# A grouped attention of 128 steps in a fused kernel: rolled rows with a drain each, or one unrolled line with another order and with the squares summed on ScalarE

## The reference, cut to what matters

```python
# x: (4, 256, 256) after layer norm; ctx: (4, 1601, 256); 16 query heads, 4 key/value heads, 128 per head
q = rms_norm((x @ Wq).reshape(4, 256, 16, 128), q_norm_w)
k = rms_norm((ctx @ Wk).reshape(4, 1601, 4, 128), k_norm_w)
v = (ctx @ Wv).reshape(4, 1601, 4, 128)
# each k and v head serves 4 query heads
probs = softmax(einsum('bqhd,bkhd->bhqk', q, k) / 128 ** 0.5)
x = x + einsum('bhqk,bkhd->bqhd', probs, v).reshape(4, 256, 2048) @ Wo
```

## Time and profile before

| what | value |
|---|---|
| median of 3 runs | 2012.29 us (2007.18 to 2012.59) |
| the profiled execution: time, span | 2008.84 us, 2007.0 us |
| busy in the span | PE 1739.7 us (87%), DVE 1303.9 us (65%), ACT 980.6 us (49%), POOL 615.8 us (31%) |
| granted TensorE clock, mean | 0.955 |
| the block: from its first DMA to its last addition | 659.9 to about 1922 us |

### The profile page before, as it was taken

The page is one execution under the profiler, slowest core; times in us unless marked ns, Lnnn a source line. Parts: engine busy times, 40 slices in busy tenths (PEclk is TensorE's granted clock), DMA queues, the critical chain, the costliest instruction groups (busy, mean ns, idle before and its releaser), DMA issues. The chain is left out here.

```text
span 2007.0 us, 32922 instructions
## 1 busy us (share of the span) xinstructions
PE 1739.7 (87%) x10769; PEld 1524.8 (76%) x10772; DVE 1303.9 (65%) x2618; ACT 980.6 (49%) x2010; POOL 615.8 (31%) x482
## 2 busy tenths in 40 slices
PE   5787599999999589998989998989998979999944
PEld 4777578888888578887878887878887868888832
DVE  3444377777776567667656677757677657676667
ACT  3333133333333255655545555545655545555536
POOL 1111054445444323223213222222222232222115
PEclk8888699999999799999999999999999999999969
DMA  3100011111110221011120100020110101010120
GB/s 103 38 33 0 21 46 39 39 39 39 39 39 14 75 65 35 17 25 23 29 56 25 28 24 25 17 69 17 25 35 17 25 22 30 14 19 17 12 76 22
DMA packets 78826, 66.90 MB, mean 33 GB/s; under 512 B 14264, under 2 KB 74208, under 8 KB 78688
## 3 DMA queue, kind: packets, MB, share of 16 engines
q1 hardware_dynamic: 78688, 65.14, 12.1%
HBM read 64.01 MB, written 1.11 MB: 32 GB/s over the span
## 5 line engine op out<-in xcount | busy, mean ns | idle before, releaser
L1420 DVE TENSOR_TENSOR ga_pT<-ga_ps_t,ga_pT 128x512 fp32r<-128x512 f32 (+1 forms) x512 | 293.0, 585 | 153.3 <-ACT ga_pT L1282 151.6
L1282 ACT ACTIVATE ga_pT<-ga_ps_t 128x512 fp32r<-128x512 f32 (+1 forms) x512 | 253.7, 518 | 206.7 <-PE ga_ps_t L1531 204.8
L1576 PE MATMUL ga_ps_m<-ga_pT,ga_v 128*128 128x512 f32 (+1 forms) x832 | 318.9, 415 | 4.6 <-DVE ga_pT L1420 4.6
L1468 PE MATMUL ga_ps_s<-ga_kT,ga_qT 128*128 128x400 f32 (+1 forms) x1536 | 313.9, 353 | 8.5 <-ACT ga_probs L1303 4.3
L1531 PE MATMUL ga_ps_t<-all_eye,ga_probs 128*128 128x128 f32 (+1 forms) x1664 | 266.4, 277 | 37.8 <-DVE ga_pT L1420 18.5
L1468 PEld LDWEIGHTS ga_ps_s<-ga_kT,ga_qT 128*128 128x128 f32 x1536 | 273.9, 189 | 15.2 <-ACT ga_probs L1303 9.0
L1303 ACT ACTIVATE ga_probs<-ga_ps_s,ga_neg_max 128x1200 f32<-128x1200 f32 (+1 forms) x256 | 238.4, 931 | 50.9 <-DVE ga_neg_max L1437 50.9
L1531 PEld LDWEIGHTS ga_ps_t<-all_eye,ga_probs 128*128 128x128 f32 (+1 forms) x1664 | 197.7, 140 | 80.5 <-DVE ga_pT L1420 32.8
L1578 PE MATMUL ga_ps_m<-ga_pT,ga_v 128*128 128x256 f32 (+1 forms) x832 | 233.4, 281 | 0.0
L1468 PE MATMUL ga_ps_t<-ga_w_in,ga_encT 128*128 128x256 f32 (+1 forms) x1248 | 176.6, 291 | 50.8 <-DVE ga_pT L1420 31.4
L1432 DVE TENSOR_REDUCE ga_part_max<-ga_ps_s 128x1 f32<-128x1200 f32 x128 | 179.5, 1402 | 47.0 <-PE ga_ps_s L1468 47.0
(11 more groups left out here) (222 smaller groups left out, 2693.0 us busy)
## 6 DMA issues: line engine op xcount, KB each, us to landing
ga_w_in_raw<-in_L_xattn_Wq SPq DMA_DIRECT2D x16, 512.0 KB, 5.3
ga_w_out_raw<-in_L_xattn_Wo SPq DMA_DIRECT2D x16, 512.0 KB, 4.6
ga_inv_rows<-ga_inv_row SPq DMA_DIRECT2D x64, 128.0 KB, 3.6
ca_cache<-in_ctx SPq DMA_DIRECT2D x4, 1536.0 KB
ga_enc<-in_ctx SPq DMA_DIRECT2D x4, 1536.0 KB
ex_raw<-in_L_ffn_Wg SPq DMA_DIRECT2D x32, 96.0 KB, 1.9
ex_raw<-in_L_ffn_Wu SPq DMA_DIRECT2D x32, 96.0 KB, 2.0
ex_raw<-in_L_ffn_Wd SPq DMA_DIRECT2D x32, 96.0 KB, 2.0
```

The costliest lines, as they stand in the source:

```text
L1282: last_one = nc.scalar.activation(dst(HI), src, ACT.Copy, scale=scale)
L1420: ins = nc.vector.tensor_tensor(dst(LO), src, f32(dst(HI)), ALU.subtract)
L1468: mm = nc.tensor.matmul(out, lhs(a), rhs(c), start=first and n == 0, stop=last and n == 2)
L1576: nc.tensor.matmul(ps_m[:, :, :], values[0:top, HI, tile, :], pT[0:top, :, tile, :], start=tile == 0, stop=False)
```

## The change

The three-times loop and the last row become one line of 128 steps and 4 that drain it. Wherever a step stands, its waits are constants. The rows overlap: the next row's first group is computed while the last probabilities of the row before are weighed. Beside that:

- ACT's square is cut per head (four pieces of 128 columns for `q`) and per tile of keys (two pieces for `kv`), each with `accum_out`, so ACT sums as it squares. The two kinds of DVE reductions of the squares go.
- The probabilities are turned for a pair of steps together, one step later than before: even steps turn the first two jobs of both, odd steps the last two (`turned_probs`). The weighing is cut in two halves, 8 tiles in odd steps and 5 in even ones (`weighed`). There are three `probs` buffers in place of two.
- Both pieces of the exponent stand behind the second ring entry of a step.
- A step's plan is: scores, two `pT`, the early entries, the weighing, two `pT`, the late entries. `y` is cut into two entries of 256 columns (steps 4 and 5).
- `q` goes to steps 0 and 1 (before: both in step 0), `q_eps` to the end of step 1, `qT` to step 2 (before: 3), the `kT` entries to step 7 (before: two in step 5, two in 7). The scaling of a pair's output on POOL stands in odd steps (before: even).
- q and output weights share one raw buffer (`w_raw`). The encoder is loaded in four parts. In the prologue keys stand before queries.

```diff
+    def turned_probs(n):
+        if n % 2 == 0:
+            u, order = n // 2 - 1, [(0, 0), (1, 0), (0, 1), (1, 1)]
+        else:
+            u, order = (n - 3) // 2, [(0, 2), (0, 3), (1, 2), (1, 3)]
+        return [("pT", (t, k), u) for t, k in order] if 0 <= u < UNITS else []
...
+    def weighed(n):
+        u, half = ((n - 3) // 2, 0) if n % 2 else (n // 2 - 2, 1)
+        return [("weigh", half, u)] if 0 <= u < UNITS else []
...
+        if to < GROUPS:
+            early, late = {
+                0: ([("q", 0, to)], []),
+                1: ([("q", 1, to)], [("q_eps", 0, to)]),
+                2: ([("qT", 0, to)], [("qT", 1, to), ("kv", 0, to)]),
+                3: ([("kv", 1, to)], [("kv", 2, to)]),
+                4: ([("kv", 3, to), ("k_eps", 0, to)], []),
+                5: ([], [("kv", 4, to)]),
+                6: ([("kv", 5, to)], [("kv", 6, to), ("k_eps", 1, to)]),
+                7: ([("kT", 0, to), ("kT", 1, to)], [("kT", 2, to), ("kT", 3, to)])}[s]
+        if 0 < g <= GROUPS and s in (4, 5):
+            late = [("y", s - 4, g - 1)] + late if s == 4 else late
+            early = [("y", s - 4, g - 1)] + early if s == 5 else early
+        row, at = divmod(g + 2, G)
+        if at == 0 and row < B:
+            late = late + {6: [("norm", 0, row)], 7: [("xT", 0, row), ("encT", 0, row), ("encT", 3, row)]}.get(s, [])
+        row, at = divmod(g + 1, G)
+        if at == 0 and row < B:
+            late = {0: [("encT", 1, row), ("encT", 4, row)], 1: [("encT", 2, row), ("encT", 5, row)],
+                    2: [("encT", 6, row), ("encT", 7, row)]}.get(s, []) + late
+        return early, late
...
-        turn = [("pT", (n - 1) * JOBS + k, 0) for k in range(JOBS)] if 1 <= n <= STEPS * G else []
-        more, to = [], g + 1
-        if n < STEPS * G and not (last and g == G - 1):
-            more = {0: [("q", 0, to), ("q", 1, to), ("q_eps", 0, to)],
-                    2: [("kv", 0, to), ("kv", 1, to), ("kv", 2, to)],
-                    3: [("qT", 0, to), ("qT", 1, to)],
-                    4: [("kv", 3, to), ("k_eps", 0, to), ("kv", 4, to)],
-                    5: [("kT", 0, to), ("kT", 1, to)],
-                    6: [("kv", 5, to), ("kv", 6, to), ("k_eps", 1, to)],
-                    7: [("kT", 2, to), ("kT", 3, to)]}.get(s, [])
-        if s == 4 and 0 < g < G:
...
+    def step_plan(n):
+        turns = turned_probs(n)
+        early, late = prepared(n) if n < N + DRAIN - 1 else ([], [])
+        if n == N + DRAIN - 1:
+            late = [("y", t, GROUPS - 1) for t in range(QT)]
+        return ([("scores", 0, n)] if n < N else []) + turns[0:2] + early + weighed(n) + turns[2:4] + late
...
+                if n % 2 and 0 <= (n - 5) // 2 < UNITS:
+                    normalize_out((n - 5) // 2)
+                for e in plan[n]:
+                    if e[0] == "norm":
+                        token_scale(e[2])
+                    if e[0] == "q_eps":
+                        query_norm(e[2])
+                    if e[0] == "k_eps":
+                        key_norm(e[1], e[2])
+                if s == 5 and g + 2 < GROUPS:
+                    split_q(g + 2)
+                if s == 7 and 0 < g < GROUPS:
+                    split_out(g)
+                if s == 7 and g + 2 < GROUPS:
+                    split_kv(g + 2)
...
+                if kind == "q":
+                    for h in range(HG):
+                        last_one = nc.scalar.activation(qn[:, m, h * DH:(h + 1) * DH],
+                                                        ps_t[:, bank_of(e), h * DH:(h + 1) * DH], ACT.Square,
+                                                        accum_out=q_sq[:, m * HG + h:m * HG + h + 1])
+                    last_one.then_inc(read, 1)
+                elif kind == "kv":
+                    at, top, src = kv_view(e)
+                    for i, tile in enumerate(kv_tiles(m)[0]):
+                        nc.scalar.activation(kn[0:top, tile, :], src[:, i, 0, :], ACT.Square,
+                                             accum_out=k_sq[0:top, tile:tile + 1])
+                    nc.scalar.activation(v[g % 2][0:top, HI, at, :], src[:, :, 1, :], ACT.Copy).then_inc(read, 1)
...
-                if kind == "q":
-                    last_one = nc.scalar.activation(qn[:, m, :], ps_t[:, bank, :], ACT.Square)
-                elif kind == "kv":
-                    tiles, top = kv_tiles(m)
-                    src = ps_t[0:top, bank, 0:len(tiles) * 2 * DH].rearrange("p (t m d) -> p t m d", m=2, d=DH)
-                    nc.scalar.activation(kn[0:top, tiles[0]:tiles[-1] + 1, :], src[:, :, 0, :], ACT.Square)
-                    last_one = nc.scalar.activation(v[p][0:top, HI, tiles[0]:tiles[-1] + 1, :], src[:, :, 1, :],
-                                                    ACT.Copy)
...
-                    a, z = EXP_AT
-                    for e in jobs[:a]:
-                        ring(row, e, e[2] % 2)
-                    if n < N_STEPS:
+            for e in prologue:
+                if e[0] == "xT":
+                    split_q(0)
+                if e[0] in RING:
+                    ring(e)
+            split_out(0)
+            split_q(1)
+            split_kv(1)
+            for n in range(N + DRAIN):
+                g, s = n // STEPS, n % STEPS
+                jobs = [e for e in plan[n] if (e[0] in RING and e[0] != "y") or e[0] == "weigh"]
+                turns = turned_probs(n)
+                if not turns and n < N:
+                    exp(n, 0)
+                    exp(n, 1)
+                for e in jobs:
+                    if e[0] != "weigh":
+                        ring(e)
+                    if turns and e == turns[1] and n < N:
                         exp(n, 0)
-                    for e in jobs[a:z]:
-                        ring(row, e, e[2] % 2)
-                    if n < N_STEPS:
                         exp(n, 1)
...
+                    if turns and e == turns[2] and n % 2 == 0 and 0 <= n // 2 - 2:
+                        take_low_part(n // 2 - 2)
+                if not turns and n % 2 == 0 and 0 <= n // 2 - 2 < UNITS:
+                    take_low_part(n // 2 - 2)
+                if n % 2 and 0 <= (n - 5) // 2 < UNITS:
+                    split_result((n - 5) // 2)
+                if s == 5 and g + 2 < GROUPS:
+                    split_q(g + 2)
+                if s == 7 and 0 < g < GROUPS:
+                    split_out(g)
+                if s == 7 and g + 2 < GROUPS:
+                    split_kv(g + 2)
...
-                    if kind == "q":
-                        nc.vector.tensor_reduce(q_sq[:, m * HG:(m + 1) * HG],
-                                                qn[:, m, :].rearrange("p (h d) -> p h d", d=DH), AX.X, ALU.add
-                                                ).then_inc(squares.sem, 1)
-                        dve.wait_ge(squares.sem, squares.level(n, m + 1))
-                        ins = nc.vector.tensor_copy(qn[:, m, :], ps_t[:, bank, :])
...
-                        nc.vector.tensor_reduce(k_sq[0:top, at], kn[0:top, at, :], AX.X, ALU.add
-                                                ).then_inc(squares.sem, 1)
-                        nc.vector.tensor_tensor(v[p][0:top, LO, at, :], src[:, :, 1, :],
-                                                f32(v[p][0:top, HI, at, :]), ALU.subtract)
-                        dve.wait_ge(squares.sem, squares.level(n, QT + m + 1))
-                        ins = nc.vector.tensor_copy(kn[0:top, at, :], src[:, :, 0, :])
```

More of the change, by code:

```diff
@@ L1070, in enc_block, with copied, emptied @@
+        def copied(e):
+            return read, read_place[e] + 1
+        def emptied(e):
+            return empty, place[e] + 1
         def enc_block(m):
@@ L1462, in _ @@
-            rows(dve, body)
+            dve.wait_ge(cleared, 4)
+            for e in prologue:
+                entry(e)
+            for n in range(N + DRAIN):
+                if n % 2 == 0 and 0 <= n // 2 - 1 < UNITS:
+                    invert(n // 2 - 1)
+                if n % 2 and 0 <= (n - 5) // 2 < UNITS:
+                    add_parts((n - 5) // 2)
+                if n < N:
+                    largest(n)
+                for e in plan[n]:
+                    entry(e)
         @block.tensor
@@ L1516, in ring @@
                 elif kind == "qT":
[L1517 removed]
+                    pe.wait_ge(q_normed, g + 1)
                     for h in range(HG):
```

827 lines of the change are left out of this document (370 added, 457 removed).

## The result

The changed kernel takes 2020.95 us (median of 6 runs, 2016.92 to 2023.0) against 2012.44 of the kernel before on the same chip: a ratio of 1.004, with a 95% interval of 1.0022 to 1.0058. It is slower by 0.4%, which is clear of the noise and still the same time when 2% is the measure. The forecast was 2016. The profiled execution took 2016.92 us in a span of 2014.8 (before: 2008.84 in 2007.0), with a mean granted clock of 0.945 (0.955).

The account below looks back on a forecast made before the run. PE was taken as the bound, the ring as second limit. From first scores to step 127's: 75.6 + 14 x 74.0 + 3 x 12.2 + 47 = 1195.2 us against 1191.5, +4, so 2016 beside the median; range 1986 to 2052.

Parts of the forecast that it names:

- query norm: Step 2, query transposes: PE waits 2.6 us for POOL, which has the output pair ahead of the norm.
- key transposes: Step 7: the second waits 1.4 us for a bank freed behind DVE's maximum, the last 1.0 for a turn's bank.
- first kv: Step 2, first kv entry: PE waits 0.85 us because its bank is the third turn's, just filled.
- short kv: Step 6, the short kv entry: PE waits 0.55 us.
- y: Step 4, the y entry: PE waits 0.2 us.
- 13.4 - 10.9: Step 2: POOL's query norm chain ends at 13.4 us, PE arrives at 10.9; the forecast called the wait 2.6.
- PE's work: Steady group of 8 steps: 66.5 us of 72.83 before, taken as unchanged because the matmuls are the same.
- the rival that took them one behind the other: ACT's small squares don't overlap their read-out, 0.47 us each: 2.1 us a group, 2047 us; chance 0.08.
- The row changes: No drain; next encoder lengthens step 7 by 4.5 us, added entries 4.7, low clock 3.0: 12.2 per row, three times.
- falls in every group: Rival: TensorE's clock falls behind step 2's wait in each group, 15 x 2.2 = 33 us: 2049; chance 0.22.
- The first group: 75.6 us against 66.8 before; step 0 takes 13.6 because q and output weights share a buffer.
- The last group: Without projections: seven steps of about 6.3 us and y, 47 us.

Follow-up runs that it names:

- e3: Changed kernel with q_eps directly behind the second q entry and POOL taking the query norm ahead of the output pair's subtraction: 1989.65 us, ratio 0.9889.
- e7: Changed kernel with the moves of e3 and e5, first output weights in a probabilities buffer, query transposes behind step 2's weighing: 1953.17 us, ratio 0.9697.
- three pairs: Small squares against squares as before, in the changed kernel, the kernel before and e8: +2.5, +2.3 and -5.1 us for the small squares.
- e8: e7 with the next row's layer norm cut in two on DVE, at the ends of steps 5 and 6: 1941.77 us, ratio 0.9642.
- e4: Changed kernel with 20 idle transposes of the unit matrix on PE in the query norm's wait: 2015.54 us, ratio 1.002.
- e9: e8 with twelve idle transposes on PE in the wait ahead of a group's first scores: 1935.09 us, ratio 0.9625.
- e10: e8 with step 7's third key transpose ahead of the weighing and the last ahead of the two later turns: 1923.32 us, ratio 0.9559.
- e5: Changed kernel with the first key transpose moved from step 7 to the end of step 5: 2003.78 us, ratio 0.9943.

## Why the prediction was right, and where it was right by luck

**The group's waits.** 7.5 us forecast, 7.5 measured, and all seven are there: query norm 2.6 (2.60), key transposes 1.4 + 1.0 (1.23 + 0.87), scores 0.85 (0.77), first kv 0.85 (0.55), short kv 0.55 (0.73), y 0.2 (0.72). The last three are off and cancel. A clean group takes 73.7 to 73.8 us, forecast 74.0. The chain behind the query norm was read rightly, down to POOL's three instructions. e3 and e7 show that it was the largest single loss: step 2 fell from 11.7 to 10.2 and to 8.7. (The forecast's own terms, 13.4 - 10.9, give 2.5 and not 2.6.)

The other term of the group is right by luck. The forecast took PE's work to be 66.5 us, from 72.83 less 6.3 of waits. But a steady group before has 5.2 us of waits, so 67.6 of work. In the changed kernel it is 66.3 (73.8 less 7.5), with the same matmuls. So the waits grew by 2.2 us a group, not by 1.2, and the rest shrank by 1.2, which the forecast did not have. Why it shrank wasn't tested.

**The squares.** Distance 0.25 us, as taken from the exponent's rows, and not 0.47. No effect of their own in three pairs. So the squares on ACT are not what moved the time. What moved it is the rest of the change, the order of steps above all. The Trainium skill (VectorE: DVE Perf Modes, The TRN2 errata) counts a fixed cost for each instruction. It speaks of instructions that read SBUF, and these squares read PSUM, but this trace agrees in so far as ACT's busy time rose by 45 us. Part of that cost overlaps here: a square of 0.28 us and its read-out of 0.21 hold ACT for 0.25 together. So the rival that took them one behind the other (2047 us) was wrong.

**The row changes.** 12.2 us each were forecast. Measured from the distances, with the slow steps taken off: 10.9, 12.2 and 12.2. Step 7 takes 16.7 to 18.1 us, forecast 18. The second one shows what the forecast described: PE stands 4.96 us ahead of the key transposes of step 7, and the granted clock from 1226.00 to 1243.36 us is 0.80. e8 shows that DVE's stand for the layer norm was part of it.

**The step that was mis-sized: the clock.** The forecast let it stay up inside the rows and gave the rival "falls in every group" 0.22. It falls in 10 of 14 groups and costs 1.4 us in each, 14 us together, where the rival had 33. The forecast's own sign for that rival, a granted clock below 0.95, came: 0.945. Its reason against the rival was that before, the wait of 2.41 us had come together with another. e4 shows that the low clock of step 2 hangs on the one wait of 2.6 us, and e9 that the one of step 0 hangs on the 1.5 us ahead of the scores: with the wait filled, those steps are never slow. (In e9 a wait of 0.6 us just ahead of it stays, and doesn't do it.) What else it takes isn't shown, since other groups with the same waits stay at 2.4 GHz. The Trainium skill (TensorE: Matmul & The Clock Gate, HAM oscillation) says that gaps which come again in each round make the clock fall and rise again and again. Its example has gaps of some 3 to 5 us. Here gaps of 2.6 us do it, but not in every round: a low clock came in 10 of 14, in seven of them behind the gap of step 2.

**What hid it.** The first group came to 71.7 us instead of 75.6: -3.9. Its step 0 took 12.5 instead of 13.6 and its step 2 was 1.0 longer, so these nearly cancel. The rest is that steps 4 and 5 of the first group have no `y`, since there is no group ahead of it: 7.0 and 7.6 us, where the later groups take 9.5 and 8.9. The forecast had overlooked that. The last group took 44.3 instead of 47: -2.7. The 14 groups between, less the clock and the row changes, took 73.71 on average: 14 x 0.29 = -4.0, and the row changes gave -1.3. Together -11.9, against +14.5 of the clock. So 1195.2 and 1197.8 lie close by cancellation. The sum's terms were off by more than the sum.

**Against the kernel before.** The drains' gain is real and is spent. From the first scores of a row to those of the next, the changed kernel takes 307.0, 311.2 and 310.1 us, the kernel before 311.9, 310.4 and 310.6. The last row is longer, 269.5 for 258.6 (to the scores of step 127), since it now begins with the last weighing and `y` of the row ahead of it, and has three slow steps. Of the changed kernel's 1197.8 us, 14 are the clock inside the rows, 5.6 the start's shared buffer, and the longer waits (7.5 for 5.2) cost 14 x 2.2 = 31. Without these, by this estimate, it would stand some 44 us below the kernel before. e10, from first to last scores 1102 us, is 90 below it, since it also removes waits that the kernel before had.

## What to carry to other kernels

When a hand-written order is redone, list for each wait of the bottleneck engine what stands queued ahead on the engine that ends it. One subtraction on POOL ahead of the query norm cost 31 us here, the clock included (e3), and the squares that gave the change its name nothing that could be told. Read waits as a set: taking one away uncovers the next (0.8 us became 1.5 in e5), so price a move by the step's new length, not by the sum of the waits it removes. Take a steady group for the waits, not the mean of a longer stretch: here that was 5.2 us against 6.3. And a short wait that comes again each round can cost half as much again by TensorE's clock (here 1.4 us behind one of 2.6). It is tested cheaply by filling it with idle matmuls.
